# A gated recurrence ahead of a mixture of experts: unhalved gate weights, tanh in two instructions in all steps, and a reordered opening

## The reference, cut to what matters

```
def step(h, xt):
    m = concatenate([xt, h]) @ weight + bias
    c = tanh(m[:, 256:])
    g = sigmoid(m[:, :256] + 1.0)
    h = g * h + (1 - g) * c
x = x + h of every step          # h starts as cond_1024
```

## Time and profile before

| | |
|---|---|
| median of 3 runs | 656.67 us |
| the profiled execution's own time | 656.54 us |
| its span | 654.8 us |
| granted TensorE clock, mean | 0.996 |
| TensorE matmul busy | 641.1 us (98%) |
| weight loads busy | 557.0 us (85%) |
| VectorE busy | 420.0 us (64%) |
| ScalarE busy | 316.1 us (48%) |
| GpSimd busy | 257.5 us (39%) |

### The profile page before, as it was taken

The page is one execution under the profiler, slowest core; times in us unless marked ns, Lnnn a source line. Parts: engine busy times, 40 slices in busy tenths (PEclk is TensorE's granted clock), DMA queues, the critical chain, the costliest instruction groups (busy, mean ns, idle before and its releaser), DMA issues.

```text
span 654.8 us, 16617 instructions
## 1 busy us (share of the span) xinstructions
PE 641.1 (98%) x5828; PEld 557.0 (85%) x5828; DVE 420.0 (64%) x950; ACT 316.1 (48%) x553; POOL 257.5 (39%) x507
## 2 busy tenths in 40 slices
PE   8899999999999999999999999999999999999995
PEld 5799888888888888888798888888888999999994
DVE  5888987666675765668677544454446775555554
ACT  5564453434344333434557444444446664454560
POOL 1557776445455445434326133203320443321200
PEclk9999999999999999999999999999999999999998
DMA  7511210000000000000003100000002310000006
GB/s 275 196 36 34 65 51 2 1 1 0 0 0 0 0 0 0 1 2 1 2 2 98 32 0 0 0 0 0 0 0 66 106 40 0 0 0 0 0 2 258
DMA packets 7752, 20.75 MB, mean 32 GB/s; under 512 B 800, under 2 KB 1056, under 8 KB 7200
## 3 DMA queue, kind: packets, MB, share of 16 engines
q1 hardware_dynamic: 7424, 19.59, 8.6%
q10 hardware_dynamic: 288, 0.64, 0.3%
HBM read 16.03 MB, written 4.19 MB: 31 GB/s over the span
## 4 chain that ended last, share of the span: by engine, by line
PE 94%; DVE 2%; DMA 1%; issue 1%; ACT 1%; POOL 0%; DVEq 0%; SPq 0%; ACTq 0%
PE zy L929 57%; PE hp L929 38%; DMA acc<-in_x 1%; DVE acc L874 0%; DVE d_t L590 0%; DVE h_b L593 0%; DVE d_t L586 0%; DVE y_all L802 0%; ACT uc L423 0%; DVEq L874 0%; POOL acc L315 0%; ACT g_hi L449 0%; ACT stage L442 0%; POOL x_hl L334 0%; ACT w_buf L449 0%
## 5 line engine op out<-in xcount | busy, mean ns | idle before, releaser
L560 DVE TENSOR_TENSOR g_lo<-g_f,g_hi 128x512 fp32r<-128x512 f32 (+2 forms) x175 | 129.5, 740 | 151.3 <-ACT g_hi L449 149.0
L929 PE MATMUL zy<-g_hi,w_buf 128*128 128x512 f32 (+2 forms) x736 | 186.5, 375 | 0.0
L449 ACT ACTIVATE g_hi<-g_f 128x512 fp32r<-128x512 f32 (+2 forms) x184 | 109.9, 597 | 151.9 <-PE zy L929 151.7
L442 ACT ACTIVATE g_f<-hp,first 128x512 f32<-128x512 f32 (+3 forms) x188 | 122.9, 654 | 117.3 <-PE hp L929 114.2
L929 PE MATMUL hp<-shared_buf,w_buf 128*128 (+1 forms) x720 | 173.6, 376 | 0.0
L929 PEld LDWEIGHTS hp<-shared_buf,w_buf 128*128 128x128 f32 x720 | 135.0, 188 | 19.1 <-issue 0.3
L929 PEld LDWEIGHTS zy<-g_hi,w_buf 128*128 128x128 f32 x736 | 132.1, 188 | 19.0 <-DVE acc L607 0.4
L929 PEld LDWEIGHTS zy<-h_b,y_all 128*128 128x128 bf16 x3072 | 93.3, 98 | 17.2 <-issue 13.1
L929 PE MATMUL zy<-g_lo,w_buf 128*128 128x512 f32 (+2 forms) x368 | 107.5, 373 | 0.0
L929 PE MATMUL hp<-x_hl,w_buf 128*128 (+2 forms) x432 | 104.9, 378 | 0.1
L929 PE MATMUL zy<-h_b,y_all 128*128 128x64 bf16 x3072 | 101.0, 193 | 2.5 <-DVE h_b L593 2.4
(11 more groups left out here) (128 smaller groups left out, 456.4 us busy)
## 6 DMA issues: line engine op xcount, KB each, us to landing
stage<-in_w_exp SPq DMA_DIRECT2D x40, 256.0 KB, 2.8
out_y<-acc SPq DMA_DIRECT2D x2, 1376.0 KB, 4.7
acc<-in_x SPq DMA_DIRECT2D x1, 2048.0 KB, 8.4
acc<-in_x SPq DMA_DIRECT2D x1, 1536.0 KB, 10.3
out_y<-acc SPq DMA_DIRECT2D x1, 1344.0 KB, 5.1
acc<-in_w SPq DMA_DIRECT2D x1, 512.0 KB, 4.7
acc<-in_x SPq DMA_DIRECT2D x1, 512.0 KB, 6.9
acc<-in_w ACTq DMA_DIRECT2D x1, 512.0 KB, 5.6
```

The lines of the kernel that those rows point to most:

```text
L442: act.activation(raw_of(j, n, keep), hp[j % 2][:, 0:n], ACT.Gelu_apprx_tanh, bias=par[:, S_B1 + e * NCH + j:S_B1 + e * NCH + j + 1]).then_ ...
L449: act.activation(chunk_of(j, n, keep)[0], raw_of(j, n, keep), ACT.Copy).then_inc(ghi_done, 1)
L560: dve.tensor_tensor(lo, raw_of(j, n, keep), hi.bitcast(F32), ALU.subtract).then_inc(glo_done, 1)
L929: return pe.matmul(out_, lhsT=lhsT, rhs=rhs, start=start, stop=stop, skip_group_check=True)
```

## The change

The gate's weights are no longer halved; the factor 0.5 moves into the gate's tanh as its scale, so the tanh is two instructions in all 64 steps. With it go the two halving instructions on wh (L473), the scaling of wx and its low parts (four and four instructions of 256 columns become two and two of 512), and the halving of the bias. The seed of steps 0 to 3 moves from VectorE to ScalarE, ahead of the copies of wx. The two halves of w0 have semaphores of their own. The DMA of the first 8 steps of x becomes two of four steps. The low part of x of steps 4 to 7 moves from GpSimd to VectorE, ahead of cell 0. The matmuls of mod move behind h_first, and mod's addition on VectorE behind cell 0; silu is kept in g_f instead of d_t. The cut diff:

```diff
-            sp.dma_start(raw_w0[:, 0:K], ...).then_inc(s_w0, 16)
-            sp.dma_start(acc[:, :, 0:GT], x[:, :, 0:GT]).then_inc(s_x0, 16)
+            sp.dma_start(raw_w0[:, 0:K], ...).then_inc(s_wx, 16)
+            sp.dma_start(acc[:, :, 0:QT], x[:, :, 0:QT]).then_inc(s_x0, 16)
+            sp.dma_start(acc[:, :, QT:GT], x[:, :, QT:GT]).then_inc(s_x4, 16)
...
# GpSimd
             pool.tensor_copy(x_hl[:, 0, :, 0:QT], acc[:, :, 0:QT]).then_inc(x0_hi, 1)
-            pool.wait_ge(x4_hi, 1)
-            pool.wait_ge(wh_split, K)
-            pool.tensor_tensor(x_hl[:, 1, :, QT:GT], acc[:, :, QT:GT], x_hl[:, 0, :, QT:GT].bitcast(F32),
-                               ALU.subtract).then_inc(xs_done, QT)
+            pool.wait_ge(xs_done, QT)
...
# ScalarE
+            def tanh(s, i, buf):
+                act.wait_ge(c_done, s + 1)
+                act.activation(uc[:, 1], zb[:, buf, 1, :, i % QT, :], ACT.Tanh).then_inc(tanh_c, 1)
+                act.wait_ge(z_done, s + 1)
+                act.activation(uc[:, 0], zb[:, buf, 0, :, i % QT, :], ACT.Tanh, scale=0.5).then_inc(tanh_done, 1)
...
             act.activation(uc[:, 0], h_f[:, 0], ACT.Tanh, scale=0.5).then_inc(silu_t, 1)
-            act.wait_ge(s_w0, 32)
+            act.wait_ge(opened, 1)
+            act.wait_ge(bias_ready, 1)
+            seed(0, seeded_first)
+            act.wait_ge(s_wx, 16)
             for k in range(K):
-                act.activation(wx[:, 0, k, 0:D], raw_w0[:, k, 0:D], ACT.Copy, scale=0.5)
-                act.activation(wx[:, 0, k, D:2 * D], raw_w0[:, k, D:2 * D], ACT.Copy).then_inc(wx_hi, 1)
+                act.activation(wx[:, 0, k], raw_w0[:, k], ACT.Copy).then_inc(wx_hi, 1)
+            act.wait_ge(s_wh, 16)
             for k in range(K):
-                act.activation(raw_w0[:, K + k, 0:D], raw_w0[:, K + k, 0:D], ACT.Copy, scale=0.5).then_inc(wh_half, 1)
-                act.wait_ge(wh_half, k + 1)
                 act.activation(wh[:, 0, k], raw_w0[:, K + k], ACT.Copy).then_inc(wh_first, 1)
-            act.wait_ge(s_x0, 16)
+            act.wait_ge(s_x4, 16)
...
# VectorE
             dve.wait_ge(s_first, 16)
+            dve.tensor_scalar(bias_z[:, 0:K], par[:, S_B0:S_B0 + K], 1.0, None, ALU.add)
+            dve.tensor_copy(bias_z[:, K:2 * K], ...).then_inc(bias_ready, 1)
...
-            dve.tensor_copy(zy[:, 0:2]..., bias_z...).then_inc(seeded_first, 1)
             for k in range(K):
                 dve.wait_ge(wx_hi, k + 1)
-                for a, scale in ((0, 0.5), (D, 1.0)):
-                    last = dve.scalar_tensor_tensor(out=wx[:, 1, k, a:a + D], ...)
-                last.then_inc(wx_split, 1)
+                dve.tensor_tensor(wx[:, 1, k], raw_w0[:, k], wx[:, 0, k].bitcast(F32), ALU.subtract).then_inc(wx_split, 1)
...
-            dve.wait_ge(mod_mm, 1)
-            dve.tensor_tensor(mod_f, hp[0][0:B, 0:8], par[0:B, S_TB:S_TB + 8], ALU.add)
+            dve.wait_ge(x4_hi, 1)
+            dve.tensor_tensor(x_hl[:, 1, :, QT:GT]..., acc[:, :, QT:GT]..., ALU.subtract).then_inc(xs_done, QT)
             for i in range(GT):
-                cell(i, i, i < 2, True)
+                cell(i, i, i < 2)
+                if i == 0:
+                    dve.wait_ge(mod_mm, 1)
+                    dve.tensor_tensor(mod_f, hp[0][0:B, 0:8], par[0:B, S_TB:S_TB + 8], ALU.add)
...
# TensorE: c_done is counted in h_part of every step, and
             x_first()
-            pe.wait_ge(silu_done, 1)
-            ... the 4 matmuls of mod
...
                         h_first()
+                        pe.wait_ge(silu_done, 1)
+                        ... the 4 matmuls of mod, from silu in g_f
```

More of the change, by code:

```diff
@@ L54 @@
 POS_AT, LIST_AT = 2, 5
-APART = GT + QT
 C_FIRST = [2, 3, 0, 1]
@@ L161, in cond_resid_kernel @@
         cmp_w = slot_w[0:B, :]
-        s_first, s_w0, s_con, s_x0, s_x1, s_x2, s_out = (
-            sem(n) for n in ("s_first", "s_w0", "s_con", "s_x0", "s_x1", "s_x2", "s_out"))
+        s_first, s_wx, s_wh, s_con = (sem(n) for n in ("s_first", "s_wx", "s_wh", "s_con"))
+        s_x0, s_x4, s_x1, s_x2, s_out = (sem(n) for n in ("s_x0", "s_x4", "s_x1", "s_x2", "s_out"))
         piece_in = [sem(f"piece_in{i}") for i in range(RING)]
@@ L170, in cond_resid_kernel @@
         opened, seeded_first, seeded = sem("opened"), sem("seeded_first"), sem("seeded")
-        wh_half, wh_first, wh_rest, wh_mid, wh_split = (
-            sem(n) for n in ("wh_half", "wh_first", "wh_rest", "wh_mid", "wh_split"))
+        wh_first, wh_rest, wh_mid, wh_split = (
+            sem(n) for n in ("wh_first", "wh_rest", "wh_mid", "wh_split"))
         x4_hi = sem("x4_hi")
@@ L414, in _, with seed @@
         def _(act):
-            def seed(buf):
+            def seed(buf, done):
                 act.activation(zy[:, 2 * buf:2 * buf + 2].rearrange("p a (m n) -> p (a m) n", m=K),
[L418 to L429, removed]
+                               bias_z.unsqueeze(2).to_broadcast([P, 2 * K, QT * B]), ACT.Copy).then_inc(done, 1)
+            def tanh(s, i, buf):
[3 more added lines that the diff above has]
+                act.activation(uc[:, 0], zb[:, buf, 0, :, i % QT, :], ACT.Tanh, scale=0.5).then_inc(tanh_done, 1)
                 if i % QT == QT - 1:
-                    if apart:
-                        act.wait_ge(tanh_c, s + 1)
+                    act.wait_ge(tanh_c, s + 1)
                     act.wait_ge(tanh_done, s + 1)
-                    seed(buf)
+                    seed(buf, seeded)
             def gelu_chunk(g, j, e, n, very_first=False, keep=False):
@@ L480, in _ @@
                 act.activation(wh[:, 1, k], raw_w0[:, K + k], ACT.Copy).then_inc(wh_mid, 1)
-            act.wait_ge(opened, 1)
-            act.wait_ge(bias_ready, 1)
-            seed(1)
+            seed(1, seeded)
             act.wait_ge(s_x1, 16)
             for i in range(GT):
-                tanh(i, i, i // QT, True)
+                tanh(i, i, i // QT)
                 for t in [GT, GT + 1] if i == 0 else [GT + i + 1]:
@@ L499, in _ @@
                 q, j = chunk_at(s // GT, i)
-                tanh(s, i, i // QT, s < APART)
-                if s < APART - 1:
+                tanh(s, i, i // QT)
+                if s < GT + QT - 1:
                     x_high(GT + s + 1)
@@ L577, in split_state, with cell @@
                 dve.tensor_tensor(h_b[:, 2], h_r[:], h_b[:, 1], ALU.subtract).then_inc(h3_done, 1)
[L579 to L584, removed]
+            def cell(s, i, first=False):
+                dve.wait_ge(tanh_c, s + 1)
                 dve.wait_ge(h_done, s + 1)
@@ L587, in cell @@
                 dve.wait_ge(d_done, s + 1)
-                if apart:
-                    dve.wait_ge(tanh_done, s + 1)
+                dve.wait_ge(tanh_done, s + 1)
                 dve.scalar_tensor_tensor(out=d_t[:], in0=uc[:, 0], scalar=1.0, in1=d_t[:],
@@ L662, in _ @@
                     shared_out(0, yp)
-                cell(s, i, apart=s < APART)
+                cell(s, i)
                 split_lo(q, j, width(q))
@@ L972, in h_first, with h_part @@
                 last.then_inc(z_done, 1)
-            def h_part(s, i, buf, apart=False):
+            def h_part(s, i, buf):
                 for a, ready in enumerate((h1_done, h2_done, h3_done)):
@@ L982, in h_part @@
                                 last = mm(o, wh[:, b, k, m * P:(m + 1) * P], h_b[:, a, k], False, a == 2)
-                        if apart and a == 2 and m == 2 * K - 1:
+                        if a == 2 and m == 2 * K - 1:
                             last.then_inc(c_done, 1)
@@ L1056, in steps @@
                         h_first()
+                        pe.wait_ge(silu_done, 1)
+                        for k in range(K):
+                            last = mm(hp[0][0:B, 0:2 * E], silu[:, k * B:(k + 1) * B], par[:, S_TW + 2 * E * k:S_TW + 2 * E * (k + 1)],
+                                      k == 0, k == K - 1)
+                        last.then_inc(mod_mm, 1)
                     else:
-                        h_part(s, i, i // QT, head is not None and s < APART)
+                        h_part(s, i, i // QT)
                     q, j = chunk_at(g, i)
```

19 lines of the change are left out of this document (8 added, 11 removed).

## The result

The changed kernel took 655.18 us (median of 20 runs, 655.08 to 655.68), the kernel before, run beside it, 656.49 us. The ratio is 0.9981 with a 95% interval of 0.9975 to 0.9987: faster, by an amount just inside the 0.2% that the prediction called "no change that can be told". 655.6 was forecast, with 655.0 to 656.5 as the range.

What follows compares the result with a forecast made beforehand. TensorE, busy 641.1 of 654.8 us, was taken as the bound, with gains only in the opening: 0.65 + 0.33 + 0.17 - 0.05 = 1.10 us, giving 655.6 us, range 655.0 to 656.5 (8 in 10).

Steps and rivals of the forecast that it cites:

- no change that can be told: Whole kernel: a time within about 0.2% of the kernel before, 655.36 to 657.98 us; chance 0.62.
- First x and the start of x_first, 0.65: Opening: x lands at 7.47 instead of 8.09, so x_first starts at 8.25 instead of 8.90, 0.65 us earlier.
- rival A: Opening: GpSimd's copy of x loses the shared ports to VectorE, x_first starts near 9.0; 656.3 us, chance 0.22.
- x_first ends 8.25 + 3.36: Opening: x_first's passes are held by nothing new and take 3.36 us, ending at 11.61.
- mod, 0.33: Opening: mod's 4 matmuls leave the path ahead of h_first, a gain of 0.33 us.
- The 0.05 set aside for it: Behind h_first: allowance for mod not fitting TensorE's queue before the next h_part; up to 0.1 us lost, 0.05 taken.
- wh in time: Opening: second and third parts of wh are ready before h_first wants them, by 0.4 and 0.2 us.
- Cell 0, 0.17: Step 0: with GpSimd's L337 gone, cell 0's L586 takes 0.30 instead of 0.47 us, a gain of 0.17.
- Tanh apart, 0: Steps 12 to 63: splitting tanh in two is worth 0, ends -1.0 to +1.0 us over 52 steps.
- Rival C: Loop: the c_done count and second wait slow TensorE in each of 52 steps; above 656.7 us, chance 0.07.
- B: Opening: rival with more gain, from shorter VectorE operations in steps 0 and 1 and earlier x_first; 655.2 us, chance 0.14.
- Later waits move with the chain: After the opening: GpSimd's sums, weight pieces and x of steps 32 to 63 move with the 1.15 us earlier h_part.

Runs made afterwards that it cites:

- e12: The changed kernel, unaltered, run once more for its trace; that execution took 655.20 us.
- traced upper run: The changed kernel's own traced execution, 655.62 us, one of the later of its two groups of run times.
- e7: The changed kernel with the low part of x of steps 4 to 7 back on GpSimd; 655.80 us.
- e4: The changed kernel with the 4 matmuls of mod back ahead of h_first; 655.66 us.
- e9: The changed kernel with the low wx made in four instructions of 256 columns again; 655.49 us.
- e2: The changed kernel with GpSimd waiting for both high wx before it copies x; 656.32 us.
- e1: The changed kernel with VectorE waiting for GpSimd's high x of steps 0 to 3 before the low wx; 655.35 us.
- e10: The changed kernel with VectorE, not GpSimd, copying the high x of steps 0 to 3 ahead of the low wx; 655.22 us.
- upper group: The 5 of the changed kernel's 20 runs that lie between 655.52 and 655.68 us.
- lower group: The 15 of the changed kernel's 20 runs that lie between 655.08 and 655.27 us, median 655.16.
- e6: The changed kernel with the first seed back on VectorE ahead of the low wx; 655.56 us.
- e3: The kernel before, weights still halved, with tanh in two instructions in all 64 steps; 656.46 us, ratio 0.9999.
- e5: The changed kernel with the DMA of x of steps 0 to 3 issued ahead of the wx half of w0 on SP; 656.55 us.

## Why the prediction was right, and where it was not

**The number and the sign.** 655.6 against 655.18; the sum was 1.10 us and the runs show 1.31. Of the 0.42 us between the two numbers 0.18 is the kernel before, 656.49 beside it instead of 656.67. The sum came out near for a mixed reason, and in part by luck: what stands in it as the start of x_first was paid through another row in most runs and hardly at all in the rest.

**First x and the start of x_first, 0.65.** Landing was put at 7.47; it is 7.41 and 7.50 in the two traces. High wx was put at 8.15, x_first at 8.25. The high wx was ready at 7.97 in e12 and 8.04 in the traced upper run. In e12 the first load is at 8.18: 0.69. In the traced upper run it is at 8.83: 0.04. That is rival A, with its place (GpSimd's copy behind VectorE's first low wx), its margin of 0.1 us, and a start near 8.9 instead of 9.0. It had 0.22 and, if each run above 655.5 is a lost race as the traced one is, happens in 5 of 20 runs, and by hundredths: GpSimd's 7.46 against VectorE's 7.49 wins, 7.55 against 7.55 loses, and in e7, e4 and e9 leads of 0.03, 0.02 and 0.01 us win. e2 forced it, e1 and e10 took it away. Its total was put too late, at 656.3 instead of 655.6, because of the next two points and the earlier kernel before.

**"x_first ends 8.25 + 3.36".** This is the step that failed. 3.36 us was not TensorE's work but work and a wait: in the kernel before, the second pass stood still for VectorE's low wx for 0.22 us, so "wanted at 9.4", taken from the first pass's 1.18 us, had the wait in it.

The passes alone are worth 0.25 us in the upper group, where the late start gives VectorE time, and 0.12 in the lower; the rest of 0.35 and 0.21 is the switch to mod. In the lower group the second pass still waits: the low wx was ready at 9.22, by 9.3 as forecast, but wanted at 9.12. The path there runs through VectorE, and the 0.69 at the first load is near the forecast 0.65 by luck. Along the path the second pass starts 0.82 us earlier (10.09 to 9.27), mod with its switch gives 0.41 and cell 0 0.14: the 1.37 of the table. What made it earlier is VectorE's time: it is free of the seed (e6, 0.4 us), has two instructions instead of four (e9, 0.2 us), and starts at 7.49 instead of 8.39. What released the first load of each pass, and not only the first of all, shows it in the trace of before.

**mod, 0.33.** Too small by 0.09, the longer switch: 0.42 is gone from the path in both traces, and e4 gets it back. TensorE's queue behind h_first did fit: x_part's loads end ahead of the h_part, which waits 0.26 us for the state. The 0.05 set aside for it was needed elsewhere: mod's addition on VectorE makes cell 1 late, whose first operation now takes 0.36 to 0.37 us instead of 0.30, and the step 3.14 us instead of 3.08.

**wh in time.** Held, with less to spare than I worked out: in e12 the third parts are ready at 12.41 and h_first's last pass wants them at about 12.5. The chain on VectorE (low wx, low x, rests, third parts, 4.9 us from 7.5) is what would be late next. That is an estimate from these rows; in e10, where x_first is 0.18 us earlier, the chain is earlier with it (third parts at 12.19).

**Cell 0, 0.17.** The step from h_first to the next h_part is 0.14 to 0.15 shorter. But the row was misread as a price. Without the move the h_part of step 1 starts at 14.67 (e7), though h_first starts at 11.22, so to the lower group the move is worth 0.5 us in the trace and 0.62 in the medians.

**Tanh apart, 0.** Right and shown by itself (e3). Rival C did not happen. The number of the lower group, 655.16, is B's (655.2), its causes are not: the gain above 1.10 comes from the low wx and mod, not from later cells.

**Later waits move with the chain.** Right: 0.85 and 1.25 us are left of 0.87 and 1.37 at VectorE's last addition; 0.05 to 0.06 was lost in step 1, and the rest is small changes either way.

**The chances.** "No change that can be told" had 0.62 and "faster" 0.33; the measured ratio of 0.9981 lies 0.0001 from that bound, so neither was far off. The working has a slip: 655.2 to 655.36 is a fifth of the forecast's width, not a third, which would have given 0.25 instead of 0.33.

## What to carry to other kernels

A stretch of matmuls between two rows of the chain is not a constant: look at what released each pass inside it before you move its start. When GpSimd and VectorE have work that becomes ready within a tenth of a microsecond, the order can come out anew in each execution. Here two groups of run times 0.4 us apart were its sign, one trace showed only one of them, and moving the short instruction to the other engine ended it. The cost of a lock read from one overlap is only what that overlap left; bound it by the whole length of the other engine's instruction. And an engine beside TensorE can set the path inside TensorE's busiest stretch: six traces agree to 0.01 us on the distance from VectorE's low wx to the h_part of step 1.

## What the runs showed of the hardware that was not expected

The same 117 KB DMA landed 4.8 us after its issue when a 512 KB transfer of weights was issued on the other queue at the same time, and 2.1 us when 256 KB of x were (e5, one trace), while the weights, now second, needed 7.0 us instead of 4.6. Why the order matters by so much more than its bytes was not tested.

The 16 opening matmuls have identical operands and no waits, and took a different time from trace to trace, at a granted clock of 1.00 (full speed, 2.4 GHz) from 2 to 9 us in both of the traces below. The changed kernel's, then e4's (duration ns min/median/max, first and last start):

```profile
L911 PE MATMUL hp<-seg x16: 379/379/634, 3.0 to 6.8; 128*128 128x512 bf16 x16
```

```profile
L911 PE MATMUL hp<-seg x16: 379/634/634, 3.0 to 8.3; 128*128 128x512 bf16 x16
```

More of them have the longer of the two durations in e4, and there they end so late that they, and no longer GpSimd's copy, release x_first. The starts of their weight loads, 0.43 us apart at first and 0.22 later, show the same change of pace: behind 4.2 us in the changed kernel, behind 7.2 in e4. What decides when the pace changes stayed open.
